# Two bias adds of a pipelined ViT-layer kernel: from selecting-row matmuls to accumulating DMAs of GpSimd, with the engines' lists ordered anew

## The chip, the cores and the metric

The kernel runs on one core of one Trainium2 chip. The metric is the device time of one execution in microseconds (us), and lower is better. All times in this document are in us unless marked ns.

## The reference

The input is a map of 64 steps x 128 rows x 64 complex states. A state-space kernel K of 1024 values for each row (computed from log_dt, B and A) is multiplied in and gives tokens `h` of 1024 values; a class token row is put beside the 128 rows. Each token then goes through an adapter (down to 128, two passes of a gated scan layer, up to 1024) and a mixture layer:

```python
h = x @ w_down.T + b_down            # after a layer norm of x; 1024 -> 128, then gelu
h = _hydra(h, *hp)                   # short causal convolution, decays, scan forward and backward,
                                     # gate silu(z), root-mean-square norm, out projection
h = alpha * xmid + (1.0 - alpha) * h
h = xmid + h
h = h @ w_up.T + b_up                # up layer, its bias is b_up
return x_init + jnp.transpose(h, (1, 0, 2))
...
base_out = jnp.einsum('btd,od->bto', x, base_W) + base_b     # base layer, its bias is base_b
logits = jnp.einsum('btd,nd->btn', x, router_W) + router_b   # 15 logits, softmax, top 8, 8 experts of rank 16
```

The output is the adapter's residual stream plus the base layer and the routed low-rank experts, computed from a second layer norm.

## The kernel before

The tokens are cut into 65 tiles of 128 (two rows of 64 steps each, `p` is the parity of the tile; the last is the class token). After a start-up block that turns and splits the weights (about 200 us), one loop body `body(i, p)` runs on each engine for i = 0 to 69, written out as straight code with a hardware loop over i = 8 to 61. It is software-pipelined over five tiles: in iteration i the engines build tile i (`A`), run the scan layer's first half for tile i-1 (`H`) and second half for tile i-2 (`G`), the up layer, residual and second norm for tile i-4 (`D`), and the base layer, router and experts for tile i-5 (`E`). What one iteration does on an engine is a list of helper calls written by hand in one order; every engine works in program order, and helpers wait on counting semaphores (`wait(eng, tile, name=count)`, `inc(ins, name)`).

What the change and the prediction touch:

- TensorE (PE): `bases(h, a, b)` multiplies parts a to b (128 of the 1024 inputs each, three 512-column matmuls a part) of the base layer into bank `bO[h]`; `route(a, b)` does the same for the expert and router columns with three 144-column matmuls a part; `lora(h)` adds the experts; `up(h)` is one half of the up layer. Before, `bases` and `up` opened their bank with a matmul of `row_sel` (two rows of ones) by `base_bias` or `up_bias`. `mix` multiplies the scan matrix `Mt` by `XS` and waits for `Mt`.
- VectorE (DVE): `gated_a` scales `XM`, the adapter input of tile i-4; `mix_matrix` writes `Mt`; `residual(h)` adds the up layer's bank to `T2` into `HB`; `final(h)` adds `bO[h]` into `HB`.
- SyncE (SP): `store` writes `HB` out after both `final`; behind it in SP's queue are the two fetches for the next iteration's `D` tile, `T2` (tokens, 512 KB) and `XM` (64 KB), whose completion is the semaphore `fetched`. `gated_a` waits for both fetches (`fetched=2`).
- GpSimd (POOL): `root_y`, `root_1`, `root_2` are powers of -0.5 for the norms, `add_bc` adds convolution taps, `carry_h` normalizes `T`, `decays_back` builds one side of the decays.

Of the kernel before, what the change touches and what calls it, by code (L numbers as in the profile page):

```python
# [26 lines left out]
ALU = mybir.AluOpType  # L27
# [27 lines left out]
def build(nc, x, cls_tok, log_dt, tok_B, inv_A_real, A_imag, w_down, b_down, w_up, b_up, gate1, in_w,  # L55
# [19 lines left out]
    with ExitStack() as keep:  # L75
# [55 lines left out]
        with ExitStack() as tmp:  # L131
# [325 lines left out]
            def _(dve):  # L457
# [128 lines left out]
                for c in range(CHUNKS):  # L586
# [89 lines left out]
                   fetched=(2, 16), up=2, h1=2, st2=4, rs2=1, nm2=1, xh2=1, tr2=2, xhi=2, xlo=2,  # L676
# [34 lines left out]
        def active(i, lag, count):  # L711
            return (not isinstance(i, int)) or 0 <= i - lag < count
# [22 lines left out]
        with nc.Block() as block:  # L735
# [64 lines left out]
            def _(pool):  # L800
                def body(i, p):
                    A, A1, D = active(i, 0, CLS), active(i, 0, TILES), active(i, 4, TILES)
                    H, G = active(i, 1, TILES + 2), active(i, 2, TILES + 2)
                    q, r, td = i - 1, i - 2, i - 4
# [97 lines left out]

                    swap()
                    kernel_q()
# [4 lines left out]
                    root_y()  # L909
                    root_1()  # L910
                    add_bc(1)
                    deviation_1()
                    add_bc(2)
                    add_bc(3)
                    add_bc(4)
                    root_2()
                    add_bc(5)
                    decays_back(0)
                    add_bc(6)
                    decays_back(1)  # L920
                    carry_h()
# [5 lines left out]
            def _(act):  # L927
# [3 lines left out]
                def body(i, p):  # L931
# [153 lines left out]

                    keep_x()
                    keep_xs()
                    exp_decays()
# [10 lines left out]
                    keep_y()  # L1099
                    exp_router()  # L1100
                    gated_hi()
# [3 lines left out]
                    exp_dt()  # L1105
# [3 lines left out]
                    scale_bc(4)  # L1109
                    scale_bc(5)  # L1110
# [3 lines left out]
                    keep_w()  # L1114
                    norm_2()
                    keep_turned(1)
# [11 lines left out]
            def _(dve):  # L1128
                TT, TS, STT = dve.tensor_tensor, dve.tensor_scalar, dve.scalar_tensor_tensor

                def body(i, p):
# [289 lines left out]
                    kernel_p()  # L1421
                    gram(0)
                    gram(1)
                    kernel_sum()
                    gram_forth()
                    gram_sum()
                    mix_matrix()
# [13 lines left out]
                    gated_a()  # L1441
                    router(0)
                    stats_1(1)
                    router(1)
                    layer_out()
                    gated_b()
                    stats_1(2)
                    conv(4, 0)
                    router(2)
                    gated_lo()  # L1450
                    stats_1(3)
                    router(3)
                    conv(4, 1)
                    conv(5, 0)
                    router(4)
                    router(5)
                    softplus(0)
                    softplus(1)
                    residual(0)
                    router(6)  # L1460
                    softplus(2)
                    shift_1()
                    softplus(3)
                    router(7)
                    stats_2(0)
                    residual(1)
                    softplus(4)
                    stats_2(1)
                    softplus(5)
                    softplus(6)  # L1470
                    conv(5, 1)
                    stats_2(2)
                    softplus(7)
                    softplus(8)
                    router(8)
                    softplus(9)
                    softplus(10)
                    softplus(11)
                    stats_2(3)
                    conv(6, 0)  # L1480
                    softplus(12)
                    shift_2()
                    conv(6, 1)
                    split_decays(0)
                    weighted_lo()
                    split_decays(1)
                    decays_forth(0)
                    decays_forth(1)
# [9 lines left out]
            def _(pe):  # L1498
                mm, tr = pe.matmul, pe.transpose

                def body(i, p):
# [6 lines left out]
                    def ffn(c0, c1, bank, ks, last=None):  # L1508

                        for k in ks:  # L1510
                            for n, (xs_, ws) in enumerate(((XHI, w_hi), (XHI, w_lo), (XLO, w_hi))):
                                ins = mm(bank[:, 0:c1 - c0], xs_[:, 1 - p, k, :], ws[:, k, c0:c1],  # L1512
                                         start=(c0 == HID and k == 0 and n == 0), stop=(last == k and n == 2))
                        return ins
# [31 lines left out]
                    def up(h):  # L1546
                        if D:
# [6 lines left out]
                            mm(bT[:, :], row_sel[:, :], up_bias[:, c], start=True, stop=False)  # L1554
                            mm(bT[:, :], GTS[:, 0, :], wu_hi[:, c], start=False, stop=False)
# [163 lines left out]
                    grams()  # L1719
                    turn_xs()  # L1720
                    decay_sums()
                    turn_x()
                    bases(0, 0, 1)
                    route(0, 1)
                    bases(1, 0, 1)
                    bases(1, 1, 2)
                    route(1, 2)
                    bases(0, 1, 2)
                    route(2, 3)
                    route(3, 4)  # L1730
                    mix()
                    s4d(0)
                    route(4, 5)
                    project_x()
                    route(5, 6)
                    s4d(1)
                    route(6, 7)
                    route(7, 8)
                    bases(0, 2, 3)
                    bases(0, 3, 4)  # L1740
                    turn_y()
                    bases(0, 4, 5)
                    bases(1, 2, 3)
# [4 lines left out]
                    bases(1, 3, 4)  # L1748
                    bases(0, 6, 7)
                    up(1)  # L1750
                    project_z()
                    bases(1, 4, 5)
                    turn_a(0)
                    bases(0, 7, 8)
                    bases(1, 5, 6)
                    turn_h()
                    bases(1, 6, 7)
                    turn_a(1)
                    bases(1, 7, 8)
# [36 lines left out]
```

How the kernel before makes its waits and increments, by code:

```python
    def after(self, eng, n, j=None):  # L48
        if isinstance(n, int) and n < 0:
            return
        j = self.per if j is None else j
        eng.wait_ge(self.sem, (n * self.per + j) * self.unit)
# [178 lines left out]
            @block.sync  # L231
# [22 lines left out]
                small(dtb[:, :], dt_bias.unsqueeze(0).broadcast_to([P, NH]))  # L254
                small(alog[:, :], A_log.unsqueeze(0).broadcast_to([P, NH]))
                small(Dbc[:, :], hy_D.unsqueeze(0).broadcast_to([P, NH]))
                small(bdn[:, :], b_down.unsqueeze(1))
                small(gate[:, :], gate1.broadcast_to([P, 1]))
                sp.wait_ge(s_zero, 3)
                for k in range(2):
                    small(bc_s[32 * k:32 * k + DST, :], in_w[2 * DIN + DST * k:2 * DIN + DST * (k + 1), :])
                    small(cwb[32 * k:32 * k + DST, :], cwr[DIN + DST * k:DIN + DST * (k + 1), :])
                    small(cbb[32 * k:32 * k + DST, :], conv_b[DIN + DST * k:DIN + DST * (k + 1)].unsqueeze(1))
                for c in range(CHUNKS):
                    sp.wait_ge(s_tab, 2 * c + 2)
                    sp.wait_ge(s_vals, 4 * c + 4)
                    sp.dma_start(tables[c * HCH // 2:(c + 1) * HCH // 2].rearrange("t f b k -> f t b k"),
                                 tab[:, c % 2, :, :].rearrange("f (t b) k -> f t b k", b=2)).then_inc(s_kept[c % 2], 16)
                for k in range(2):
                    sp.wait_ge(s_kept[k], 16 * CHUNKS // 2)
# [428 lines left out]
        def inc(ins, name):  # L700
            ins.then_inc(S[name].sem, S[name].unit)
```

## Time and profile before

| what | value |
|---|---|
| median of 3 runs | 2343.29 us (2339.07 to 2344.38) |
| the profiled execution's own time | 2339.94 us |
| its span in the trace | 2338.2 us |
| TensorE busy in the span | 2161.3 us (92%) |
| DVE, ACT, POOL busy | 1847.3, 1528.2, 1091.2 us |

TensorE's 92% is an average over a start-up of some 200 us, in which it does little, and the tile loop. The loop is read by itself in the views below. A matmul's "busy" time in the trace includes its pipeline depth, so the time that one takes from the next is the distance of two starts, not the duration printed.

### The profile page before, as it was taken

What the parts mean: (1) busy time and instruction counts of PE and PEld (TensorE: products, weight loads), DVE (VectorE), ACT (ScalarE), POOL (GpSimd) and SP (SyncE); (2) the same over time, 40 slices, a digit from 0 to 9 for tenths busy, and PEclk for the clock granted to TensorE, in tenths of its full rate; (3) what the DMA queues carried; (4) which work ended last, traced back from release to release, by engine and by line L of the source; (5) the groups of instructions that cost most, each with busy time, mean ns of one, the idle gap of its engine ahead of it and who ended that gap; (6) DMA issues with size and microseconds to landing.
All of it is one profiled execution on the core that took longest, in us unless ns stands there. A gap on an engine that the chain in (4) does not pass through costs nothing.

```text
span 2338.2 us, 51899 instructions
## 1 busy us (share of the span) xinstructions
PE 2161.3 (92%) x14117; PEld 1805.6 (77%) x14117; DVE 1847.3 (79%) x4980; ACT 1528.2 (65%) x2921; POOL 1091.2 (47%) x1350
## 2 busy tenths in 40 slices
PE   1356799999999999999999999999999999999998
PEld 1245688888888888888888888888888888888776
DVE  6847688888888888888888888888888888888764
ACT  2546576766677766667666767666777666676652
POOL 2534355444455444455444554444554444554331
PEclk9756799999999999999999999999999999999999
DMA  4400122112222122221122221122211222211211
GB/s 92 117 29 24 35 64 64 42 54 63 63 63 61 35 61 63 63 63 48 47 63 63 63 63 40 55 63 63 63 58 36 63 63 63 63 47 47 69 39 33
DMA packets 90061, 132.61 MB, mean 57 GB/s; under 512 B 20379, under 2 KB 63559, under 8 KB 90006
## 3 DMA queue, kind: packets, MB, share of 16 engines
q1 hardware_dynamic: 79176, 125.60, 18.2%
q10 hardware_dynamic: 10830, 6.35, 1.1%
q8 instruction: 25, 0.41, 0.1%
q14 instruction: 30, 0.25, 0.0%
HBM read 55.17 MB, written 76.74 MB: 56 GB/s over the span
## 4 chain that ended last, share of the span: by engine, by line
issue 43%; PE 27%; POOL 9%; DVE 7%; ACT 6%; POOLq 1%; DVEq 0%; ACTq 0%; DMA 0%; SPq 0%
PE bank L1611 5%; PE bank L1512 5%; POOL CB L901 4%; PE bank L1567 3%; PE bank L1542 2%; DVE NF L1241 2%; ACT L1006 2%; POOL XD L852 2%; PE bank L1685 1%; PE bank L1669 1%; POOL RS L886 1%; PE bank L1544 1%; PE bank L1543 1%; POOL RS L865 1%; PE bank L1659 1%
## 5 line engine op out<-in xcount | busy, mean ns | idle before, releaser
L1512 PE MATMUL bank<-w_hi,XHI 128*128 128x512 f32 (+1 forms) x1560 | 622.9, 399 | 0.0
L1512 PE MATMUL bank<-w_lo,XHI 128*128 128x512 f32 (+1 forms) x1560 | 554.7, 356 | 0.0
L1512 PE MATMUL bank<-w_hi,XLO 128*128 128x512 f32 (+1 forms) x1560 | 554.4, 355 | 0.0
L1147 DVE SCALAR_TENSOR_TENSOR CX<-bank,cw,CX 128x252 f32<-128x252 f32 (+5 forms) x804 | 335.7, 460 | 61.8 <-ACT CX L944 61.6
L901 POOL TENSOR_TENSOR CB<-CB,CM 48x252 f32<-48x252 f32 (+5 forms) x402 | 292.7, 728 | 153.6 <-ACT CM L929 142.7
L1512 PEld LDWEIGHTS bank<-w_hi,XLO 128*128 128x128 f32 x1560 | 295.5, 189 | 46.9
L1512 PEld LDWEIGHTS bank<-w_lo,XHI 128*128 128x128 f32 x1560 | 296.8, 190 | 41.4
L1512 PEld LDWEIGHTS bank<-w_hi,XHI 128*128 128x128 f32 x1560 | 296.4, 190 | 41.2
L929 ACT ACTIVATE T<-bank 64x512 f32<-64x512 f32 x256 | 151.4, 592 | 261.1 <-PE bank L1601 256.5
L865 POOL TENSOR_TENSOR RS<-VE,half_neg 128x1 f32<-128x1 f32 x65 | 35.5, 546 | 369.9 <-DVE VE L1339 369.9
L892 POOL TENSOR_TENSOR RB<-m_gt,AS 128x512 fp32r<-128x512 f32 x134 | 164.9, 1231 | 56.8 <-DVE AS L1413 56.8
L929 ACT ACTIVATE CM<-CR,cwb 48x256 f32<-48x256 f32 x402 | 181.5, 497 | 3.7 <-POOL CB L901 1.5
L859 POOL TENSOR_TENSOR RS<-MS,half_neg 128x2 f32<-128x2 f32 x67 | 46.9, 700 | 242.8 <-DVE MS L1270 242.8
L1601 PE MATMUL bank<-VB,W 128*128 128x256 f32 x512 | 148.9, 415 | 7.4 <-DVE W L1212 5.2
L1395 DVE TENSOR_TENSOR XLO<-bank,XHI 128x512 fp32r<-128x512 f32 x130 | 89.9, 692 | 72.1 <-ACT XHI L929 72.1
L1401 DVE TENSOR_TENSOR RF<-m_lt,AS 128x512 fp32r<-128x512 f32 x134 | 142.9, 1105 | 0.0
L1611 PE MATMUL bank<-XHT,wdT 128*128 128x128 f32 x1040 | 135.8, 287 | 4.5 <-ACT XHT L929 4.5
L929 ACT ACTIVATE XHI<-bank 128x512 fp32r<-128x512 f32 x130 | 77.6, 597 | 94.7 <-PE bank L1567 94.7
L1611 PEld LDWEIGHTS bank<-XHT,wdT 128*128 128x128 f32 x1040 | 129.4, 203 | 6.1 <-ACT XHT L929 6.1
L844 POOL TENSOR_TENSOR NB<-GB,sp_dt 128x512 f32<-128x512 f32 x67 | 95.9, 1431 | 77.4 <-DVE GB L1224 77.4
L852 POOL TENSOR_TENSOR XD<-XS,DD 128x512 f32<-128x512 f32 x67 | 84.6, 1263 | 99.0 <-DVE DD L1232 54.2
L1601 PEld LDWEIGHTS bank<-VB,W 128*128 128x128 f32 x512 | 89.9, 196 | 23.1 <-issue 5.9
(295 smaller groups left out, 5332.5 us busy)
## 6 DMA issues: line engine op xcount, KB each, us to landing
carried<-T SPq DMA_DIRECT2D x65, 512.0 KB, 4.8
T<-carried SPq DMA_DIRECT2D x65, 512.0 KB, 3.9
out<-HB SPq DMA_DIRECT2D x129, 256.0 KB, 3.2
tables<-tab SPq DMA_DIRECT2D x8, 560.0 KB, 4.3
TB<-tables SPq DMA_DIRECT2D x64, 70.0 KB, 2.7
carried<-U SPq DMA_DIRECT2D x65, 64.0 KB, 3.6
XM<-carried SPq DMA_DIRECT2D x65, 64.0 KB, 4.8
XI<-in_x SPq DMA_DIRECT2D x128, 32.0 KB, 2.8
```

The lines of the kernel that those rows point to most:

```text
L844: inc(pool.tensor_tensor(NB[:, :, :].rearrange("p (a h) t -> p a h t", a=2), GB[:, :, :].unsqueeze(2).broadcast_to([P, 2, NH, CS]), dtB, A ...
L852: inc(pool.tensor_tensor(XD[:, :, :], v3(XS[:, :], HD), DD[:, :].unsqueeze(2).broadcast_to([P, 2 * NH, HD]), ALU.mult), "xd")
L892: inc(pool.tensor_tensor(RB[:, part, :, :], m_gt[:, :].unsqueeze(1).broadcast_to([P, 2 * NH, CS]), decays(1, part), ALU.mult), "rb")
L901: inc(pool.tensor_tensor(CB[:, :, s:CS], CB[:, :, s:CS], CM[:, s % 3, :, 0:CS - s], ALU.add), "cbc")
L929: inc(act.activation(dst, src, ACT.Copy, scale=scale), name)
L1147: inc(STT(CX[:, c, :, s:CS], src[:, :, 0:CS - s], cw[:, c, k:k + 1], CX[:, c, :, s:CS], ALU.mult, ALU.add), "conv")
L1395: inc(TT(XLO[:, p, ks, :], v3(bT[:, :], P), XHI[:, p, ks, :].bitcast(F32), ALU.subtract), "xlo")
L1401: inc(TT(RF[:, part, :, :], m_lt[:, :].unsqueeze(1).broadcast_to([P, 2 * NH, CS]), decays(0, part), ALU.mult), "rf")
L1512: ins = mm(bank[:, 0:c1 - c0], xs_[:, 1 - p, k, :], ws[:, k, c0:c1], start=(c0 == HID and k == 0 and n == 0), stop=(last == k and n == 2))
L1567: ins = tr(bT[:, P * k:P * (k + 1)], T2[:, (4 * g + k) * P:(4 * g + k + 1) * P], ident[:, :])
L1601: ins = mm(bK[:, 256 * s:256 * (s + 1)], W[:, b, 2 * s:2 * s + 2, :].rearrange("p a c -> p (a c)"), VB[:, b, :, :].rearrange("p a c -> p ( ...
L1611: ins = mm(bK[:, 0:P], wdT[:, k, :], XHT[:, k, :], start=(k == 0), stop=(k == KC - 1))
```

## The change

Each of the two biases is now added by a DMA that GpSimd issues with an accumulating write: `bias_up` adds `b_up`, broadcast over 128 partitions, into `T2` once that is fetched; `bias_base` adds `base_b` into `HB` once the second norm has read it. `residual` waits for the first (`upb=1`), `final` for the second (`baseb=1`). The four selecting-row matmuls of an iteration go. The lists of GpSimd, ScalarE, VectorE and TensorE are written in a new order; SyncE's list is as it was. The start-up work that builds `row_sel`, `up_bias` and `base_bias` stays.

```diff
+                    def bias_up():
+                        if D:
+                            wait(pool, td, fetched=2)
+                            apart(pool)
+                            inc(pool.dma_start(T2[:, :], b_up.unsqueeze(0).broadcast_to([P, HID]), accum_op=ALU.add), "upb")
+
+                    def bias_base():
+                        if E:
+                            wait(pool, te, xh2=1)
+                            apart(pool)
+                            inc(pool.dma_start(HB[:, 1 - p, :], base_b.unsqueeze(0).broadcast_to([P, HID]),
+                                               accum_op=ALU.add), "baseb")
...
                     root_y()
+                    bias_base()
+                    bias_up()
                     root_1()
...
                     def residual(h):
-                            wait(dve, td, up=h + 1, fetched=2)
+                            wait(dve, td, up=h + 1, upb=1)
...
                     def final(h):
-                            wait(dve, te, o=h + 1)
+                            wait(dve, te, o=h + 1, baseb=1)
...
                     gram_sum()
+                    gated_a()
                     mix_matrix()
...
-                                mm(bO[h][:, :], row_sel[:, :], base_bias[:, HALF * h:HALF * (h + 1)], start=True, stop=False)
...
-                            mm(bT[:, :], row_sel[:, :], up_bias[:, c], start=True, stop=False)
-                            mm(bT[:, :], GTS[:, 0, :], wu_hi[:, c], start=False, stop=False)
+                            mm(bT[:, :], GTS[:, 0, :], wu_hi[:, c], start=True, stop=False)
```

VectorE's list, in the first body of the hardware loop, before the change, from the sum of the scan matrix (`NF`) to the first products that read `XM`:

```order
L1247 TENSOR_TENSOR NF<-NF,NB 128x512 [waits nb,nf]
L1254 TENSOR_TENSOR Mt<-NF,EX 128x512 [waits yy,ex,ns]
L1206 TENSOR_TENSOR W<-XTC,TB 128x2x192 [waits km,xtc]
L1232 TENSOR_TENSOR DD<-bank,Dbc 128x8 [waits xd,gram]
...
L1331 BN_STATS ST<-T 128x6 [waits hev]
L1352 TENSOR_SCALAR XM<-XM,al 128x128 [waits fetched]
L1297 TENSOR_TENSOR LG<-bank,rbias 128x15 [waits se,rt]
```

and the same place now:

```order
L1238 TENSOR_TENSOR GF<-bank,m_lt 128x2x63 [waits nf,nb,gram]
L1241 TENSOR_TENSOR GB<-bank,m_gt 128x2x63 [waits nf,nb,gram]
L1210 TENSOR_TENSOR VB<-TB 128x512 [waits km,x_in_even]
L1258 TENSOR_TENSOR NF<-GF,sp_dt 128x512 [waits mm,outp,g4]
L1216 TENSOR_TENSOR VB<-VB,V 128x512 [waits v1,v2]
L1264 TENSOR_TENSOR NF<-NF,NB 128x512 [waits nb,nf]
L1369 TENSOR_SCALAR XM<-XM,al 128x128 [waits fetched]
L1271 TENSOR_TENSOR Mt<-NF,EX 128x512 [waits yy,ex,ns]
L1223 TENSOR_TENSOR W<-XTC,TB 128x2x192 [waits km,xtc]
```

The scaling of `XM` (`gated_a`) moved from behind the convolution taps to the place right ahead of `Mt` (`mix_matrix`); the six instructions ahead of it are those that stood ahead of `Mt` before, in another order.

GpSimd's list around the power for the output norm (`RS<-MS`, `root_y`), before:

```order
L852 TENSOR_TENSOR XD<-XS,DD 128x512 [waits yn,tyn,dd,xse]
L859 TENSOR_TENSOR RS<-MS,half_neg 128x2 [waits yn,ms]
L865 TENSOR_TENSOR RS<-VE,half_neg 128x1 [waits sd1,xh1,st1]
L901 TENSOR_TENSOR CB<-CB,CM 48x4x63 [waits cbm]
L873 TENSOR_SCALAR SD<-RS 128x1 [waits rs1,tt]
```

and now:

```order
L852 TENSOR_TENSOR XD<-XS,DD 128x512 [waits yn,tyn,dd,xse]
L859 TENSOR_TENSOR RS<-MS,half_neg 128x2 [waits yn,ms]
L894 DMA HB<-in_L_ffn_base_b 128x1024 [waits xh2]
L887 DMA T<-in_L_attn_b_up 128x1024 [waits fetched]
L865 TENSOR_TENSOR RS<-VE,half_neg 128x1 [waits sd1,xh1,st1]
```

The two DMAs stand between `root_y` and `root_1`, the base layer's first (names are printed without buffer numbers: `T` there is `T2`).

TensorE's list just ahead of `mix` (the `Mt` row), now:

```order
L1634 MATMUL bank<-ident,XI 128x128
L1635 MATMUL bank<-ident,XSW 128x128
L1529 MATMUL bank<-w_hi,XHI 128x512
L1529 MATMUL bank<-w_lo,XHI 128x512
L1529 MATMUL bank<-w_hi,XLO 128x512
L1529 MATMUL bank<-w_hi,XHI 128x144
...
L1712 MATMUL bank<-XS,Mt 64x64 x16
```

Between `lora` and `mix` there stood two selecting-row matmuls, four base parts and four router parts; now five base parts and two router parts stand there, and the turning of `XI` comes three base parts and a router part later.

## Rows read from the trace of the kernel before

**Rows 1.** The page: span, and busy time of each engine

```profile
span 2338.2 us, 51899 instructions
PE 2161.3 (92%) x14117; PEld 1805.6 (77%) x14117; DVE 1847.3 (79%) x4980; ACT 1528.2 (65%) x2921; POOL 1091.2 (47%) x1350
```

**Rows 2.** Busy time in a stretch of the tile loop, then granted clock, DMA share

```profile
core 0: us, PE busy (x) PEld busy (x) DVE busy (x) ACT busy (x) POOL busy (x), PEclk, DMA share, GB/s
1000.00:1500.00 500.00, 497.34 (x3346) 418.81 (x3345) 414.41 (x1132) 348.12 (x665) 248.39 (x298) 1.00 0.20 59
```

**Rows 3.** Timeline of PE over one iteration: start, duration, line, operation

```profile
1000.33 0.60 PE L1578 MATMUL bank<-ident,H 128*128 128x128 f32 x4
...
1003.90 0.40 PE L1512 MATMUL bank<-w_hi,XLO 128*128 128x512 f32 x1
1004.37 0.50 PE L1542 MATMUL bank<-lb_hi,HWS 128*128 128x512 f32 x1
...
1005.87 0.60 PE L1567 MATMUL bank<-ident,T 128*128 128x128 f32 x4
...
1015.80 0.28 PE L1512 MATMUL bank<-w_hi,XHI 128*128 128x144 f32 x1
1015.91 0.28 PE L1512 MATMUL bank<-w_lo,XHI 128*128 128x144 f32 x1
...
1016.23 1.15 PE L1697 MATMUL bank<-XS,Mt 64*64 64x64 f32 x32
...
1027.57 0.51 PE L1554 MATMUL bank<-up_bias,row_sel 128*128 128x512 f32 x1
...
1030.00 0.39 PE L1554 MATMUL bank<-up_bias,row_sel 128*128 128x512 f32 x1
1030.23 0.39 PE L1555 MATMUL bank<-wu_hi,GTS 128*128 128x512 f32 x1
...
1032.48 0.60 PE L1578 MATMUL bank<-ident,H 128*128 128x128 f32 x4
```

**Rows 4.** Timeline of DVE in the same iteration

```profile
1007.74 1.28 DVE L1419 TENSOR_TENSOR HB<-bank,HB 128x512 f32<-128x512 f32 x2
...
1013.37 1.21 DVE L1247 TENSOR_TENSOR NF<-NF,NB 128x512 f32<-128x512 f32 x1
1014.72 0.69 DVE L1254 TENSOR_TENSOR Mt<-NF,EX 128x512 f32<-128x512 f32 x1
...
1024.69 0.27 DVE L1352 TENSOR_SCALAR XM<-XM,al 128x128 f32<-128x128 f32 x1
...
1029.03 0.69 DVE L1368 TENSOR_TENSOR HB<-bank,T 128x512 f32<-128x512 f32 x1
```

**Rows 5.** Timeline of SP's queue in the same iteration

```profile
1009.24 1.23 SPq L793 DMA_DIRECT2D out<-HB  x2
1010.97 0.36 SPq L759 DMA_DIRECT2D T<-carried  x1
1011.51 0.58 SPq L760 DMA_DIRECT2D XM<-carried  x1
```

**Rows 6.** DMA issues of the run: count, KB, median us to landing

```profile
T<-carried SPq DMA_DIRECT2D x65, 512.0 KB, 3.9
...
TB<-tables SPq DMA_DIRECT2D x64, 70.0 KB, 2.7
...
XM<-carried SPq DMA_DIRECT2D x65, 64.0 KB, 4.8
...
T<-in_cls_tok SPq DMA_DIRECT2D x1, 512.0 KB, 5.7
```

**Rows 7.** Timeline of POOL in the same iteration, idle time and releaser in brackets

```profile
1020.98 0.70 POOL L859 TENSOR_TENSOR RS<-MS,half_neg 128x2 f32<-128x2 f32 x1 [3.53 <-DVE MS L1270]
1027.31 0.55 POOL L865 TENSOR_TENSOR RS<-VE,half_neg 128x1 f32<-128x1 f32 x1 [5.63 <-DVE VE L1339]
```

**Rows 8.** Timeline of SP's queue at the class-token tile

```profile
2167.09 0.38 SPq L768 DMA_DIRECT2D carried<-T  x1
2167.57 0.42 SPq L748 DMA_DIRECT2D T<-in_cls_tok  x1
```

More of the change, by code:

```diff
@@ L915, in body @@
                     add_bc(4)
+                    add_bc(5)
+                    add_bc(6)
                     root_2()
-                    add_bc(5)
                     decays_back(0)
-                    add_bc(6)
+                    carry_h()
                     decays_back(1)
-                    carry_h()
                 iterations(pool, body)
@@ L1109, in body @@
                     scale_bc(4)
+                    exp_dt()
                     scale_bc(5)
@@ L1114, in body @@
                     keep_w()
+                    keep_turned(1)
                     norm_2()
-                    keep_turned(1)
                     silu_x()
@@ L1440, in body @@
                     stats_1(0)
-                    gated_a()
+                    stats_1(1)
+                    gated_b()
+                    layer_out()
                     router(0)
-                    stats_1(1)
+                    stats_1(2)
                     router(1)
-                    layer_out()
-                    gated_b()
-                    stats_1(2)
+                    gated_lo()
+                    stats_1(3)
                     conv(4, 0)
                     router(2)
-                    gated_lo()
-                    stats_1(3)
+                    conv(4, 1)
                     router(3)
-                    conv(4, 1)
-                    conv(5, 0)
                     router(4)
                     router(5)
+                    router(6)
                     softplus(0)
+                    residual(0)
                     softplus(1)
-                    residual(0)
-                    router(6)
+                    shift_1()
+                    conv(5, 0)
+                    residual(1)
+                    router(7)
+                    router(8)
+                    stats_2(0)
                     softplus(2)
-                    shift_1()
+                    stats_2(1)
                     softplus(3)
-                    router(7)
-                    stats_2(0)
-                    residual(1)
+                    conv(5, 1)
                     softplus(4)
-                    stats_2(1)
                     softplus(5)
+                    stats_2(2)
                     softplus(6)
-                    conv(5, 1)
-                    stats_2(2)
+                    stats_2(3)
                     softplus(7)
+                    conv(6, 0)
                     softplus(8)
-                    router(8)
                     softplus(9)
+                    shift_2()
                     softplus(10)
+                    weighted_lo()
                     softplus(11)
-                    stats_2(3)
-                    conv(6, 0)
                     softplus(12)
-                    shift_2()
-                    conv(6, 1)
                     split_decays(0)
-                    weighted_lo()
                     split_decays(1)
                     decays_forth(0)
+                    conv(6, 1)
                     decays_forth(1)
@@ L1512, in ffn @@
                                 ins = mm(bank[:, 0:c1 - c0], xs_[:, 1 - p, k, :], ws[:, k, c0:c1],
-                                         start=(c0 == HID and k == 0 and n == 0), stop=(last == k and n == 2))
+                                         start=(k == 0 and n == 0), stop=(last == k and n == 2))
                         return ins
@@ L1719, in body @@
                     grams()
+                    decay_sums()
+                    bases(1, 0, 1)
                     turn_xs()
-                    decay_sums()
+                    bases(0, 0, 1)
+                    bases(1, 1, 2)
+                    route(0, 1)
                     turn_x()
[L1723 to L1726, printed above, removed]
+                    bases(0, 1, 2)
                     route(1, 2)
-                    bases(0, 1, 2)
-                    route(2, 3)
-                    route(3, 4)
+                    bases(1, 2, 3)
                     mix()
                     s4d(0)
+                    bases(0, 2, 3)
+                    route(2, 3)
+                    project_x()
+                    route(3, 4)
                     route(4, 5)
-                    project_x()
+                    s4d(1)
+                    bases(0, 3, 4)
                     route(5, 6)
-                    s4d(1)
                     route(6, 7)
-                    route(7, 8)
-                    bases(0, 2, 3)
-                    bases(0, 3, 4)
                     turn_y()
                     bases(0, 4, 5)
-                    bases(1, 2, 3)
+                    route(7, 8)
                     project_out()
@@ L1748, in body @@
                     bases(1, 3, 4)
+                    bases(1, 4, 5)
+                    up(1)
                     bases(0, 6, 7)
-                    up(1)
                     project_z()
-                    bases(1, 4, 5)
                     turn_a(0)
-                    bases(0, 7, 8)
[L1755 to L1759, printed above, removed]
+                    bases(1, 5, 6)
+                    bases(1, 6, 7)
+                    bases(1, 7, 8)
+                    turn_h()
+                    turn_a(1)
+                    bases(0, 7, 8)
                     lora(0)
```

21 lines of the change are left out of this document (10 added, 11 removed).

## The prediction

> **What bounds the kernel now.** I read the page first for the engines' shares, then a stretch of the tile loop by itself, then one iteration on each engine, and last the DMA landings. The page gives TensorE 92% of the span and VectorE 79% [rows 1]. In a stretch of 500 us inside the loop TensorE is busy for 497.3 us at the full granted clock (1.00, the 2.4 GHz level), VectorE for 414 us, ScalarE 348, GpSimd 248 [rows 2]. So TensorE's own list sets the pace, and the others wait for it. One iteration lasts 1032.48 - 1000.33 = 32.15 us, from one turning of `H` to the next [rows 3]. TensorE is not wholly free of waits: `lora` starts 0.47 us after the last base matmul where two 512-column matmuls start 0.23 us apart, so about 0.2 us of each iteration is a wait for VectorE's `HWS` [rows 3].
>
> The reader should keep three distances in mind. From the end of `lora` (1005.87, where the turning of `T` starts) TensorE needs 10.36 us to reach `mix` at 1016.23 [rows 3]. VectorE finishes `Mt` at 1014.72 + 0.69 = 1015.41, so `mix` has 0.8 us to spare today [rows 3, 4]. And `gated_a` scales `XM` only at 1024.69 [rows 4], long after the fetch that SP issues at 1011.51 [rows 5] has landed, 4.8 us later in the median [rows 6].
>
> **What is removed.** Four selecting-row matmuls of 512 columns, two in `up` and two in `bases`. The one at 1030.00 is followed by the next start at 1030.23 [rows 3]: 0.23 us each, 0.94 us an iteration (the four taken at 0.235). Where such a matmul follows a group of another kind its start distance is longer (1027.57), but the matmul behind it inherits that. VectorE's weighted experts (`HWS`) move ahead of the splitting of the decays and a base part now stands last ahead of `lora`, so I also credit the 0.2 us wait. If nothing else ended later, an iteration would take 32.15 - 0.94 - 0.2 = 31.0 us.
>
> **What `gated_a` costs in its new place.** It waits for both fetches, and it now stands ahead of `mix_matrix`, so behind it on VectorE stand `Mt`, the shift products that `s4d` waits for, the skip scale, `add_skip` and the gate, that is, everything that leads to `mix` and to the output norm. The six instructions ahead of it are the old ones permuted, so VectorE gets there when it got to the end of the `NF` sum, 1013.37 + 1.21 = 1014.6 [rows 4]. SP cannot fetch sooner than now: its list is unchanged, and the two fetches queue behind the store, which waits for both `final`s (1007.74 + 1.28 = 1009.02); the store goes at 1009.24, `T2` at 1010.97, `XM` at 1011.51 [rows 4, 5]. All of this hangs on the end of `lora`, through the turning of `T`, its copy and VectorE's `XLO`, and the lists keep that order. So `XM` lands at 1011.51 + 4.8 = 1016.3. Then 0.27 us for the scaling, 0.69 us for `Mt` and about 0.1 us on each side: `mix` can start at 1017.4, 11.5 us after `lora`'s end.
>
> TensorE arrives earlier. Between `lora` and `mix` it loses two selecting-row matmuls (0.47 us); two router parts leave (six 144-column matmuls, 0.11 us apart by the starts at 1015.80 and 1015.91, 0.66 us) and one base part comes (three at 0.23, 0.69 us) [rows 3]. That is 10.36 - 0.47 + 0.03 = 9.9 us. It waits 11.5 - 9.9 = 1.6 us. `s4d` and `mix` are in order behind this and nothing later makes it up, since VectorE, POOL and ACT start their next work from `mix`. The iteration becomes 31.0 + 1.6 = 32.6 us, 0.45 us more than now. Over the 60 iterations in which the scan, the up layer and the base layer are all in work (i = 5 to 64) that is +27 us. In the filling and draining iterations TensorE has few base parts and other chains set the end; I cost those at nothing. If the landing were at 4.2 us instead of 4.8, the sum would be -9 us; at 5.4 it would be +63.
>
> **The two DMAs.** The issue itself falls into a hole. POOL finishes `root_y` at 1020.98 + 0.70 = 1021.7 and is then idle for 5.63 us until `root_1` is released [rows 7]. No row shows what a DMA issue costs on GpSimd. Below, it is SP's 0.36 us [rows 5]; above, both must fill the hole before `root_1` is late, 2.8 us each. I take 0.6 us each, near SP's rows, and nothing on the path. `bias_base` is wanted by `final` some 18 us later, so its landing costs nothing.
>
> `bias_up` is the tight one. It is issued second, and `residual(0)` wants it at 1029.03 in today's clock [rows 4], 7.3 us after `root_y`'s end. `up(0)` starts at 1027.57 [rows 3] and loses its 0.23 us, but VectorE gets to `residual(0)` only slightly earlier than now, so I allow 7.1 us from the first issue. Late by more than that, `residual(0)` holds `up(1)` on TensorE (it waits for `h1`), the router's sums, `shift_1`, `norm_1` and the next turning, one for one. The nearest row is the class token's load: 512 KB, the same broadcast of one 4 KB row over 128 partitions, issued 0.48 us behind another 512 KB DMA, landing 5.7 us after its issue [rows 6, 8]. With one issue of 0.6 us ahead that gives 6.3 us: in time by 0.8. That row is of a plain copy. An accumulating write has to read `T2` or `HB` as well. A plain 512 KB fetch lands after 3.9 us and a 70 KB one after 2.7 [rows 6], so 442 KB are worth 1.2 us and 512 KB 1.4; a second read of that size for each of the two DMAs makes 6.3 + 2.8 = 9.1 us, 2.0 us late, +120 us over 60 iterations. Both ends stand in the range. I take the plain copy's row, since it is the only one with this source and a DMA queued ahead.
>
> The Trainium skill speaks against that choice: "Collectives: The Full Stack", section "The bandwidth ceiling: the fold count and why AG ≠ RS ≠ AR", says that an adding transfer emits two source reads where a copy emits one, both on the same read ring, and so moves half the bytes a second; no row of this trace has an accumulating DMA. By its rule the sum would be the late end, about 2490. The Trainium skill's page "DMA: Bandwidth & Descriptors", section "Anatomy of one DMA — SWDGE (gpsimd) path", fits a GpSimd DMA by 2.0 us plus its bytes at 436 GB/s; by an estimate from that fit the pair with doubled reads would take 6.8 us plus the first issue, right at the limit.
>
> **The sum.** Per iteration -0.94 (matmuls) -0.2 (`HWS` wait) +1.6 (`XM`) +0.0 (issue, landing) = +0.45 us, times 60 = +27. The profiled execution took 2339.9 us, its span 2338.2; with the change 2367. The median of the runs stands 3.4 above the profiled one: 2370, and 2372 with a little for the bias DMAs' traffic beside others.
>
> **The rivals.**
> - *Both waits* (0.38): `XM` and a late `bias_up`. For it: the extra read, and two DMAs one behind the other. Against it: the class-token row is itself slowed by traffic around it. From barely late to 2.0 us late it gives 2385 to 2490; were the accumulating rate lower still, more.
> - *No wait at `gated_a`, the full saving* (0.12): this ends on the other side. The mechanism: the wait for `XM` is 1.6 us only if the fetch lands 4.8 us after its issue; if it lands by 3.2 us (1014.7), `gated_a` passes at once. The `XM` fetch lands later than the eight times larger `T2` fetch ahead of it [rows 6], so it is slowed by what shares the queues; a `final` about 1.6 us earlier against `mix` would do as well. Then an iteration takes 31.0 to 31.1 us, and the time is 2343 - 1.1 x 60 = 2277. It decides from a combined shift of 1.6 us on; the point where the kernel breaks even is a wait of 1.14 us instead of 1.6.
> - *A partial wait that just cancels the saving* (0.06): 2339 to 2348.
> - *`XM` alone* (0.44), my forecast: 2350 to 2385.
>
> **How the numbers follow.** What a measurement of this kernel can tell from no change is about 0.2%, 4.7 us. Slower by more: 0.44 + 0.38 less a sliver of each, 0.81. Within 0.2%: 0.06. Faster: 0.13. The range of 8 in 10 runs from 2335 to 2485: it holds the partial wait, my forecast and the both-waits case but for its last 0.08, and leaves out the full saving (0.12).
>
> **What the profile of the changed kernel would show.** VectorE's `XM` scaling with an idle time of about 1.6 us ahead of it, released by a DMA, right ahead of `Mt`; TensorE idle ahead of `mix` (released by `Mt`) by the same amount, so that its busy share in the loop falls from 99.5% to about 95%; 32.6 us from one turning of `H` to the next; `lora` no longer behind a wait for `HWS`. If `bias_up` is late, `residual(0)` is released by a DMA and `up(1)` by `HB`. I am wrong in sign if `XM` lands ahead of VectorE's arrival, and wrong in size by 1 us an iteration for each microsecond that `bias_up` lands later than 7.1 us after the first issue.

## The result, and the profile after

| | before | after |
|---|---|---|
| median of 4 runs | 2342.18 us | 2470.88 us (2461.75 to 2471.77) |
| ratio | | 1.0542, 95% interval 1.0514 to 1.057 |
| profiled execution, its span | 2339.94, 2338.2 us | 2470.55, 2468.8 us |

The change makes the kernel 5.4% slower, 129 us. It lies inside the forecast range (2335 to 2485) and on the forecast side, but the forecast value, 2372, had only 30 us of it.

The page of the changed kernel, busy time of each engine, DMA queues and what was read from HBM:

```profile
span 2468.8 us, 51958 instructions
PE 2143.9 (87%) x13857; PEld 1767.0 (72%) x13857; DVE 1770.1 (72%) x4980; ACT 1524.2 (62%) x2921; POOL 1169.0 (47%) x1480
...
q0 software_dynamic: 18720, 68.17, 14.9%
...
HBM read 123.33 MB, written 76.74 MB: 81 GB/s over the span
```

TensorE has 260 matmuls less (4 x 65) and 17 us less of busy time than in [rows 1], while the span is 131 us longer: it waits. The chain that ended last names for what, by line:

```profile
DMA T<-in_L_attn_b_up 17%; DMA XM<-carried 11%; DVE HB L1436 3%; POOL XD L852 3%; SPq L793 3%; PE bank L1529 2%; DVE CX L1164 2%; ACT XHI L946 2%; DVE HB L1385 1%; SPq L759 1%; POOL CB L916 1%; PE bank L1616 1%; POOL HB L894 1%; DVE ST L1392 1%; DVEq L52 1%
```

The same stretch of the loop as [rows 2] (busy time of PE, PEld, DVE, ACT, POOL, then granted clock, DMA share, GB/s), and the waits from 800 to 1500 us (total us, times, longest us):

```profile
1000.00:1500.00 500.00, 463.76 (x3055) 384.00 (x3054) 375.58 (x1082) 328.66 (x631) 247.92 (x310) 0.99 0.34 84
```

```profile
DVE XM L1369 <- DMA XM<-carried: 53.3, 20, 3.2
...
PE bank L1712 <- DVE Mt L1271: 33.5, 20, 2.2
...
PEld bank L1570 <- DVE HB L1385: 16.6, 20, 1.7
...
DVE HB L1385 <- DMA T<-in_L_attn_b_up: 15.2, 18, 1.7
```

TensorE's share falls from 99.5% to 93%. In about 20 iterations VectorE waits 2.7 us each for the `XM` fetch, TensorE 1.7 us each for `Mt` behind it, VectorE 0.8 us for the DMA that adds `b_up`, and the weights of the second half of `up` 0.8 us for the residual. One iteration shows the first wait; VectorE's timeline, with idle time and releaser in brackets, answers to [rows 4]:

```profile
1022.45 0.68 DVE L1264 TENSOR_TENSOR NF<-NF,NB 128x512 f32<-128x512 f32 x1
1025.84 0.29 DVE L1369 TENSOR_SCALAR XM<-XM,al 128x128 f32<-128x128 f32 x1 [2.71 <-DMA XM<-carried]
1026.04 0.68 DVE L1271 TENSOR_TENSOR Mt<-NF,EX 128x512 f32<-128x512 f32 x1
1026.64 0.55 DVE L1223 TENSOR_TENSOR W<-XTC,TB 128x384 f32<-128x384 f32 x1
```

TensorE's timeline of the same iteration (end of `lora`, then `mix`, then `s4d`), as in [rows 3]:

```profile
1015.30 0.60 PE L1582 MATMUL bank<-ident,T 128*128 128x128 f32 x4
...
1024.81 0.40 PE L1529 MATMUL bank<-w_hi,XLO 128*128 128x512 f32 x1
1026.87 1.15 PE L1712 MATMUL bank<-XS,Mt 64*64 64x64 f32 x32 [1.66 <-DVE Mt L1271]
1028.24 1.10 PE L1616 MATMUL bank<-VB,W 128*128 128x256 f32 x4 [0.22 <-issue]
```

`mix` starts 11.57 us after `lora`'s end, where the prediction had 11.5. GpSimd's timeline with the two DMAs, against [rows 7], and their landings (count, KB, median us from issue to landing), against [rows 6]:

```profile
1031.81 0.70 POOL L859 TENSOR_TENSOR RS<-MS,half_neg 128x2 f32<-128x2 f32 x1 [3.05 <-DVE MS L1287]
1032.46 0.92 POOL L894 DMA_DIRECT2D HB<-in_L_ffn_base_b  x1
1033.09 1.19 POOL L887 DMA_DIRECT2D T<-in_L_attn_b_up  x1
1037.76 0.57 POOL L865 TENSOR_TENSOR RS<-VE,half_neg 128x1 f32<-128x1 f32 x1 [3.48 <-DVE VE L1356]
```

```profile
T<-in_L_attn_b_up POOLq DMA_DIRECT2D x65, 512.0 KB, 7.2
HB<-in_L_ffn_base_b POOLq DMA_DIRECT2D x65, 512.0 KB, 5.1
...
XM<-carried SPq DMA_DIRECT2D x65, 64.0 KB, 4.8
```

The issues cost GpSimd about 0.6 us (the distance of their two starts) and 1.2 us, and lie in its hole, which still leaves 3.5 us idle. The up bias lands 0.63 + 7.2 = 7.8 us after the first issue; the limit was put at 7.1 us.

For the experiments I divided each iteration at six marks on TensorE: the turning of `T` behind `lora`, `mix`, the first `s4d`, `project_x`, `up(0)` and `up(1)` (of each, the first matmul that reads `GTS`, the up layer's input). The table has the mean distance of those starts in us, over the 44 to 48 iterations between 500 and 2000 us of each profiled run:

| kernel | lora to mix | mix to s4d | s4d to project_x | project_x to up(0) | up(0) to up(1) | up(1) to lora | iteration | time, us |
|---|---|---|---|---|---|---|---|---|
| before | 10.29 | 1.08 | 1.26 | 9.33 | 2.32 | 7.79 | 32.07 | 2342 |
| after | 11.63 | 1.44 | 2.23 | 8.27 | 2.77 | 7.82 | 34.16 | 2471 |
| e1_gated_back | 9.92 | 1.10 | 1.95 | 8.25 | 2.86 | 7.84 | 31.93 | 2332 |
| e2_up_first | 11.48 | 1.39 | 2.22 | 8.28 | 2.19 | 7.71 | 33.26 | 2416 |
| e3_both | 9.92 | 1.11 | 1.94 | 8.27 | 2.19 | 7.69 | 31.12 | 2276 |
| e4_old_lists_dma | 9.83 | 1.17 | 1.49 | 8.95 | 2.61 | 8.38 | 32.43 | 2365 |
| e5_new_lists_matmul | 11.55 | 1.35 | 1.93 | 8.61 | 2.32 | 7.57 | 33.32 | 2413 |
| e6_old_lists_up_first | 9.83 | 1.16 | 1.48 | 8.95 | 2.21 | 8.25 | 31.90 | 2327 |
| e7_plain_copy | 11.50 | 1.40 | 2.45 | 8.27 | 2.19 | 7.70 | 33.52 | 2424 |
| e8_xm_first | 9.98 | 1.13 | 1.94 | 8.36 | 2.19 | 7.70 | 31.29 | 2290 |
| e9_both_xm_first | 9.96 | 1.11 | 1.95 | 8.35 | 2.18 | 7.71 | 31.25 | 2285 |
| e10_new_lists_gated_back_matmul | 10.39 | 1.11 | 1.94 | 8.61 | 2.32 | 7.57 | 31.95 | 2322 |

(The new lists have a base part between `s4d` and `project_x` where the old ones have none, so those two columns compare only within old or new lists.)

### The profile page after: what moved, and what is told of

It reads as the page before. It is cut to its first block, busy times and chain, and to the rows that moved or that the text cites. A ratio compares the mean times of both kernels' runs of the same rounds, so it can differ in the third digit from the quotient of the medians.

```text
span 2468.8 us, 51958 instructions
## 1 busy us (share of the span) xinstructions
PE 2143.9 (87%) x13857; PEld 1767.0 (72%) x13857; DVE 1770.1 (72%) x4980; ACT 1524.2 (62%) x2921; POOL 1169.0 (47%) x1480
## 3 DMA queue, kind: packets, MB, share of 16 engines
q1 hardware_dynamic: 79176, 125.60, 17.2%
## 4 chain that ended last, share of the span: by engine, by line
DMA 28%; issue 26%; DVE 16%; PE 9%; POOL 7%; SPq 5%; ACT 4%; DVEq 1%; POOLq 0%; ACTq 0%
DMA T<-in_L_attn_b_up 17%; DMA XM<-carried 11%; DVE HB L1436 3%; POOL XD L852 3%; SPq L793 3%; PE bank L1529 2%; DVE CX L1164 2%; ACT XHI L946 2%; DVE HB L1385 1%; SPq L759 1%; POOL CB L916 1%; PE bank L1616 1%; POOL HB L894 1%; DVE ST L1392 1%; DVEq L52 1%
## 5 line engine op out<-in xcount | busy, mean ns | idle before, releaser
L916 POOL TENSOR_TENSOR CB<-CB,CM 48x252 f32<-48x252 f32 (+5 forms) x402 | 263.8, 656 | 203.1 <-ACT CM L946 164.2
L1712 PE MATMUL bank<-XS,Mt 64*64 64x64 f32 x2144 | 83.5, 231 | 108.5 <-DVE Mt L1271 108.5
L1616 PE MATMUL bank<-VB,W 128*128 128x256 f32 x512 | 156.9, 434 | 19.8 <-DVE W L1229 13.6
L1712 PEld LDWEIGHTS bank<-XS,Mt 64*64 64x64 f32 x2144 | 75.7, 144 | 135.0 <-issue 135.0
L1385 DVE TENSOR_TENSOR HB<-bank,T 128x512 f32<-128x512 f32 x130 | 89.9, 692 | 81.4 <-DMA T<-in_L_attn_b_up 45.9
L1369 DVE TENSOR_SCALAR XM<-XM,al 128x128 f32<-128x128 f32 x65 | 18.6, 286 | 164.9 <-DMA XM<-carried 164.9
L828 POOL TENSOR_TENSOR WI<-XTC,TB 128x384 f32<-128x384 f32 x64 | 55.7, 870 | 164.3 <-ACT XTC L946 164.3
```

The source lines that it names most:

```text
L916: inc(pool.tensor_tensor(CB[:, :, s:CS], CB[:, :, s:CS], CM[:, s % 3, :, 0:CS - s], ALU.add), "cbc")
L1616: ins = mm(bK[:, 256 * s:256 * (s + 1)], W[:, b, 2 * s:2 * s + 2, :].rearrange("p a c -> p (a c)"), VB[:, b, :, :].rearrange("p a c -> p ( ...
L1712: ins = mm(bX[rows, HD * k:HD * (k + 1)], Mt[rows, k, :], XS[rows, HD * k:HD * (k + 1)], start=True, stop=True)
```

## The experiments

**Theory 1**: two separate waits, for the `XM` fetch at `gated_a` and for the up bias at `residual(0)`, take more than the matmuls give. **Theory 2**: the accumulating DMAs themselves, by issue and traffic, are the loss, the wait for `XM` included. A third: the new order alone is the loss.

### e1: gated_a back behind stats_1(0)

```diff
                     gram_sum()
-                    gated_a()
                     mix_matrix()
...
                     stats_1(0)
+                    gated_a()
                     stats_1(1)
```

> The changed kernel with one line moved back: gated_a (the scaling of XM, which waits for the fetch) stands behind stats_1(0) again, as before the change. Theory 1 (the wait for XM ahead of Mt is the larger loss, with the waits of s4d and project_x that follow from a late Mt): the 1.7 us ahead of mix and the 0.7 us behind it go, 2.4 us x 62 = 150 us, so about 2320 us; what stays is the late bias_up. Theory 2 (the accumulating DMAs themselves are the loss: late landing, their issue on GpSimd, their traffic slowing the XM fetch): the wait moves elsewhere and the time stays near 2440 us.

Measured 2332.18 us (2331.01 to 2337.61), ratio to before 0.9957 (0.9941 to 0.9974): 139 us less than the changed kernel. `lora` to `mix` falls by 1.71 us, and the two distances behind `mix` by 0.34 and 0.28. The expectation was 2320. The single move accounts for more than the whole slowdown. Theory 2, which had the time near 2440, fails here: the DMAs are all still there, and the `XM` wait did not move elsewhere. What is left of it is the late up bias, next.

### e2: the up bias issued first

```diff
                     def bias_base():
                             wait(pool, te, xh2=1)
+                            wait(pool, te - 1, baseb=1)
...
                     root_y()
+                    bias_up()
                     bias_base()
-                    bias_up()
                     root_1()
```

> The changed kernel with bias_up issued ahead of bias_base (and bias_base waiting in addition for the bias_base of the tile before, long landed). Theory 1: bias_up no longer queues behind the base bias, lands some 2.7 us sooner than now after the first issue, and the 0.6 us wait ahead of up(1) goes: 0.6 x 62 = 35 us, about 2435 us; the wait for XM stays. Theory 2: most of the loss goes, below 2380 us.

Measured 2415.79 us (2405.86 to 2426.48), ratio 1.0315 (1.0274 to 1.0356): 55 us less than the changed kernel, where 35 were expected. `up(0)` to `up(1)` falls from 2.77 to 2.19 us, `lora` to `mix` stays at 11.5. The landings, count, KB and median us:

```profile
T<-in_L_attn_b_up POOLq DMA_DIRECT2D x65, 512.0 KB, 5.1
HB<-in_L_ffn_base_b POOLq DMA_DIRECT2D x65, 512.0 KB, 7.2
```

They have changed places: whichever goes second lands 7.2 us after its issue. For the base bias that costs nothing: from 500 to 2000 us of e3, which has the same order, no wait for it is listed.

### e3: both

> Both edits together. Theory 1: the two waits are separate and add up, 2471 - 150 - 35 = about 2285 us, below the kernel before (2342) by the four matmuls: 0.94 us x 62 = 58 us. Theory 2: the DMAs' issue and traffic keep it above 2342 us.

Measured 2276.3 us (2275.25 to 2277.68), ratio 0.9712 (0.9696 to 0.9728). The two waits are separate and add up: 2470.9 - 138.7 (e1) - 55.1 (e2) = 2277.1, measured 2276.3. That the two agree within 1 us is partly luck, since e2's four runs lie 20 us apart; e1 less e3, with runs within 7 us, gives 55.9 us for the late up bias as well. With both gone the change is worth 66 us, 2.9%, the fastest kernel of this study. Its page, and the stretch of [rows 2], in which TensorE is as full as before the change:

```profile
span 2275.9 us, 51985 instructions
PE 2097.2 (92%) x13857; PEld 1750.0 (77%) x13857; DVE 1778.9 (78%) x4980; ACT 1524.9 (67%) x2921; POOL 1188.2 (52%) x1480
```

```profile
1000.00:1500.00 500.00, 497.40 (x3356) 416.89 (x3355) 412.42 (x1174) 359.31 (x692) 276.56 (x339) 1.00 0.38 92
```

### e4 and e6: the old lists with the DMAs

Both leave every list of the kernel before as it was, take the four matmuls out and put the two DMAs behind `root_y`; e4 with the base bias first, e6 with the up bias first.

```diff
                     root_y()
+                    bias_base()      # e6: bias_up() first, and bias_base's extra wait as in e2
+                    bias_up()
                     root_1()
```

> The kernel before with all its lists as they were, and only the biases exchanged: the four selecting-row matmuls out, bias_base and then bias_up issued right behind root_y. Theory 1: no wait for XM; the matmuls give 0.94 us and the late bias_up takes 0.5 to 0.7 us back, about 2325 us. Theory 2: as slow as the changed kernel or nearly, above 2400 us. A third theory (the new order of the lists is the whole loss and the DMAs are free): about 2285 us.

Measured 2364.75 us (2360.79 to 2370.92), ratio 1.0095 (1.0073 to 1.0117): slower than before, by 22 us, and 40 above what theory 1 gave. So the third theory fails: without any reordering the DMAs do not give their saving. Against e6 below, the late up bias costs these lists 38 us, less than the 55 of the new ones. The 40 us above theory 1 are therefore not the bias: e6 misses by the same amount.

> The lists of the kernel before, the biases by DMAs behind root_y, bias_up ahead of bias_base (bias_base waits in addition for the one of the tile before). Theory 1: bias_up lands 5.1 us after its issue, ahead of residual(0), so every trace of the wait goes, also the 0.6 us that e4_old_lists_dma lost behind up(1): 32.07 - 0.94 = 31.1 us an iteration, about 2283 us. If the 0.6 us come from the issue on GpSimd or from traffic, they stay: about 2320 us.

Measured 2326.66 us (2325.95 to 2333.29), ratio 0.9945 (0.9927 to 0.9963): 44 above theory 1. The wait at `residual(0)` is gone (2.21), yet 0.46 us of the 0.94 saved are given back between `up(1)` and `lora` (7.79 to 8.25). The waits of e6 from 800 to 1500 us say for what in part:

```profile
PEld bank L1559 <- DVE HWS L1298: 17.3, 22, 0.8
...
PE bank L1559 <- DVE HWS L1298: 7.7, 22, 0.4
```

In the old lists VectorE writes `HWS` behind the splitting of the decays; TensorE, now faster, arrives at `lora` before it. From the start of the last base matmul to that of `lora` it takes 0.47 us before the change, 0.75 us in e4 and e6, 0.40 in e3 and 0.28 in e10 in the mean. So 0.28 of the 0.77 us that e6 gives back are this wait, which the new lists do not have. Another 0.30 us go between `mix` and `project_x` (1.16 + 1.48 against 1.08 + 1.26), for which no wait of a matmul is listed. That the matmuls' saving needs the new order is shown by e6 against e3; that it is the move of `HWS` alone was not tried.

### e5 and e10: the new lists with the matmuls

e5 has all four lists in the new order, with the selecting-row matmuls and without any DMA of GpSimd; e10 also has `gated_a` back.

> All four lists in the new order, but the biases added by the four selecting-row matmuls as before the change, and no DMA from GpSimd. Theory 1 (gated_a's wait for XM sets when mix can start, whatever adds the biases): lora's end to mix stays 11.5 us as in e2_up_first, and the other 21.8 us of its iteration gain the two matmuls of up, 0.47 us: 33.26 + 0.47 = 33.7 us, about 2445 us, some 100 above the kernel before. Theory 2 (the DMAs' traffic and issue cause the wait): 2342 us or below.

Measured 2413.01 us (2410.06 to 2414.05), ratio 1.0302 (1.0285 to 1.0319). The expectation was 32 us too high, but the sign and the place are theory 1's: without a single DMA on GpSimd, `lora` to `mix` is 11.55 us and the kernel is 71 us slower than before. Its waits:

```profile
DVE XM L1352 <- DMA XM<-carried: 53.4, 21, 3.2
...
PE bank L1697 <- DVE Mt L1254: 22.6, 21, 1.6
```

VectorE waits as long as in the changed kernel. TensorE waits 1.1 us instead of 1.7 (1.5 in e2), since its selecting-row matmuls fill part of the time: removing them ahead of a `mix` that comes late gains nothing there. e2, the same lists with the DMAs and without the late up bias, takes 2416 us, no less than e5's 2413: with `gated_a` in this place the exchange of matmuls for DMAs is worth nothing.

> All lists in the new order but gated_a at its old place, and the biases by the four selecting-row matmuls. Theory 1: this is e3_both with the four matmuls back, 0.94 us x 65 = 61 us more: 2276 + 61 = about 2337 us, the kernel before within 0.3%. If the new order is worth something by itself with TensorE full, it is below 2330; if the DMAs cost something hidden in e3_both, it is nearer to 2300.

Measured 2322.18 us (2320.11 to 2332.88), ratio 0.9929 (0.9908 to 0.9951): the new order without `gated_a`'s move is worth 18 us, and the exchange of the matmuls for DMAs 46 us (against e3; 31.95 to 31.12 = 0.83 us an iteration), less than the 61 expected. Of the 0.94 us 0.12 come back as the wait for `HWS` ahead of `lora` (0.28 to 0.40 us). The 18 us lie for the most part outside the columns, where the pipeline fills: in the profiled executions the fourth `mix` starts at 279.4 us before the change and at 267.2 in e10, 12 us sooner; the iterations from there to the sixty-first give only 0.12 us each.

### e7: the same bytes, copied and not added

```diff
-                            inc(pool.dma_start(T2[:, :], b_up.unsqueeze(0).broadcast_to([P, HID]), accum_op=ALU.add), "upb")
+                            inc(pool.dma_start(up_bias[:, :].bitcast(F32), b_up.unsqueeze(0).broadcast_to([P, HID])), "upb")
```

and the same for `base_b` into `base_bias`, two tiles that are no longer read, each DMA waiting in addition for its own of the tile before. The output lacks both biases.

> The changed kernel, but the two DMAs of GpSimd copy the same 512 KB broadcasts into two tiles that nobody reads, with no accumulation: both biases are left out of the output, all waits stay. Theory A (an accumulating write reads its destination too, so it moves half as fast): each DMA loses 1.3 us of data time, the second lands some 4.6 us after its issue instead of 7.2, at twice the GB/s while both move, and the wait ahead of residual(0) goes: about 2416 us, as e2_up_first. Theory B (the fixed time of a GpSimd DMA, or the one-row source in HBM, makes it late): landing stays 6.5 to 7.2 us and the time near 2465 us.

Measured 2423.83 us, one run. `up(0)` to `up(1)` is 2.19 us as in e2: copied, the second DMA is in time. The landings:

```profile
up_bias<-in_L_attn_b_up POOLq DMA_DIRECT2D x65, 512.0 KB, 4.9
base_bias<-in_L_ffn_base_b POOLq DMA_DIRECT2D x65, 512.0 KB, 3.9
```

And the DMA while the pair moves, us by us, in the changed kernel (last two columns: share of the 16 engines, GB/s that they moved):

```profile
1034.00:1035.00 1.00, 1.00 (x8) 0.91 (x8) 1.00 (x4) 0.95 (x3) 0.28 (x1) 1.00 0.95 123
1035.00:1036.00 1.00, 1.00 (x8) 0.91 (x7) 1.00 (x2) 0.30 (x1) 0.00 (x0) 1.00 1.09 217
1036.00:1037.00 1.00, 1.00 (x6) 0.65 (x4) 0.61 (x3) 0.03 (x1) 0.00 (x0) 1.00 1.09 213
1037.00:1038.00 1.00, 0.95 (x7) 0.69 (x6) 1.00 (x7) 0.67 (x3) 0.24 (x1) 1.00 1.02 201
1038.00:1039.00 1.00, 1.00 (x5) 0.61 (x4) 0.90 (x6) 0.58 (x2) 0.52 (x2) 1.00 1.07 209
1039.00:1040.00 1.00, 1.00 (x6) 0.82 (x5) 0.56 (x4) 0.97 (x3) 0.13 (x1) 1.00 0.45 86
```

and in e7:

```profile
1020.00:1021.00 1.00, 1.00 (x7) 0.82 (x6) 1.00 (x3) 0.97 (x3) 0.20 (x1) 1.00 0.53 188
1021.00:1022.00 1.00, 1.00 (x12) 1.00 (x10) 1.00 (x4) 0.97 (x2) 0.00 (x0) 1.00 0.99 303
1022.00:1023.00 1.00, 1.00 (x8) 0.87 (x7) 1.00 (x4) 0.60 (x1) 0.00 (x0) 1.00 1.01 401
1023.00:1024.00 1.00, 1.00 (x7) 0.90 (x7) 0.58 (x1) 0.00 (x0) 0.00 (x0) 1.00 0.40 156
```

With all engines busy the accumulating pair moves the biases at 201 to 217 GB/s, the copying pair at 303 to 401. Over the whole pair the shares add up to 5.7 and 2.9 us of all 16 engines: the accumulating write takes 1.9 times the engine time for the same bytes. That is theory A's rate, and its size too: 7.2 against 4.9 us for the second. The Trainium skill ("Collectives: The Full Stack", section "The bandwidth ceiling: the fold count and why AG ≠ RS ≠ AR") puts an adding transfer at two source reads, and so at half the rate of a copy. This trace agrees with the half; whether the second read or the adding itself takes the time, no run here separates. The time is 8 us above e2's median and inside the span of e2's runs (2405.86 to 2426.48); see the clock, below.

### e8 and e9: XM fetched ahead of T2

```diff
-                        inc(sp.dma_start(T2[:, :], src[:, 0:HID]), "fetched")
-                        inc(sp.dma_start(XM[:, :], src[:, HID:HID + P]), "fetched")
+                        inc(sp.dma_start(XM[:, :], src[:, HID:HID + P]), "xmf")
+                        inc(sp.dma_start(T2[:, :], src[:, 0:HID]), "fetched")
```

with `gated_a` waiting for `xmf=1` and `bias_up` for `fetched=1`; e8 on e2, e9 on e3.

> e2_up_first with gated_a still ahead of Mt, but SP fetches XM (64 KB) ahead of T2 (512 KB), on a semaphore of its own. Theory 1: XM is late because it is issued 0.54 us later and queues behind 512 KB: now it lands some 3 us after an issue 0.54 us sooner, about 1.5 us of the 2.4 us wait on VectorE that counts goes, with half of the waits that follow a late Mt: about 2300 to 2330 us. If what delays it is the store ahead of both, or the write of carried<-T behind them, it stays above 2380 us.

Measured 2289.96 us (2284.9 to 2290.87), ratio 0.9774 (0.9758 to 0.979): 126 us less than e2 and 10 below the expected range, with `gated_a` still right ahead of `Mt`. Landings:

```profile
T<-carried SPq DMA_DIRECT2D x65, 512.0 KB, 4.7
...
XM<-carried SPq DMA_DIRECT2D x65, 64.0 KB, 2.4
```

Issued first, the 64 KB land after 2.4 us instead of 4.7, and 0.54 us earlier besides: 2.8 us in all, a little more than the 2.4 us (51.3 us in 21 waits) that VectorE waited for them in e2. So the wait was one for 64 KB issued behind 512 KB in one queue. What stands behind `XM` now lands later: `T2` 4.7 us after its issue instead of 3.9, and `TB` 3.3 instead of 2.7. The store ahead of both and the write behind them, the rivals that the expectation named, are unchanged.

> e3_both (gated_a at its old place, bias_up first) with XM fetched ahead of T2 as in e8_xm_first. Theory 1: gated_a already stands long behind the landing, so fetching XM sooner gives nothing: 2276 us, within 0.3%. If the T2 fetch, now landing 4.7 us after its issue and later by 0.54 us, held bias_up, it would be slower.

Measured 2285.23 us (2284.49 to 2287.71), ratio 0.9762 (0.9745 to 0.9778): not the 2276 expected, 9 us slower than e3. `project_x` to `up(0)` is 0.08 us longer and `lora` to `mix` 0.04. The only wait of a matmul that is listed from 500 to 2000 us, in e3 and then in e9:

```profile
PE bank L1652 <- DVE U L1304: 4.6, 24, 0.2
...
PE bank L1652 <- DVE U L1304: 8.6, 24, 0.4
```

The 4 us more, over 48 iterations, are the 0.08 us: in every second iteration `project_bc`, which stands between the two marks, waits longer for `U`. Why VectorE writes `U` later when `T2` and `TB` land later is not shown; it stays open.

## Why the prediction was right or wrong

The direction was right, the size was not: +30 us forecast, +129 measured. By terms: the matmuls and the `HWS` wait, -68 forecast and -64 measured (e10 and e3); the `XM` wait, +96 and +139; the late up bias, nothing and +55. The last two terms are the miss. That the first agrees so well is partly luck: 10 to 12 us of the 64 come from the filling of the pipeline (the fourth `mix` in e3 and e10), which I had "at nothing".

- **What bounds the kernel, and the period.** Right: 32.15 was 32.07 in the mean. Without the two waits I gave 31.0 us; e3 has 31.12.
- **"The wait for `HWS`", -0.2, and the four matmuls, -0.94.** Together -1.14 forecast and -0.95 measured (32.07 to 31.12). The parts: the new order gives 0.12 and the matmuls 0.83 (e10). The wait for `HWS` shrank by 0.2 us, as credited, only while the matmuls stayed (e10, 0.47 to 0.28 us); with TensorE earlier it is 0.40 (e3). What I did not see is that the 0.94 depends on the new order: in the old lists (e6) TensorE gains only 0.17 us.
- **`gated_a`, +1.6.** The mechanism, the place and the stall were right: 1.56 us (e2 less e3, `lora` to `mix`). VectorE itself waits 2.7 us where the prediction had 1.7 (1016.3 - 1014.6), since it ends the `NF` sum 7.8 us after `lora` and not 8.7; that earlier arrival only lengthens its wait. The term was undersized by what follows. I took the stall as passed on one for one ("nothing later makes it up") and put nothing on top: behind a late `Mt` the shift products come late too, so `s4d` starts another 0.28 us later, and 0.28 us in the mean go to TensorE's clock (below). In all 2.14 us an iteration, 139 us instead of 96 (1.6 x 60). The factor was short as well: 139.5 / 2.14 = 65 iterations by the medians, and 134.2 / 2.14 = 63 between the two profiled executions, from which the 2.14 is.
- **The step that failed: "I take the plain copy's row".** The row of the class-token load gave 6.3 us for the landing of the up bias after the first issue, in time by 0.8, and so a term of 0.0; it was 7.8, late by 0.7, and the term 55 us. The bound for a second read gave 9.1, and the truth lay between: each accumulating write takes 1.2 us more than a copy (e7: 5.1 against 3.9 alone, 7.2 against 4.9 behind another), but the plain pair is also faster than that row (0.63 + 4.9 = 5.5 us). Why, no run shows; the row is a single load, and it took 4.9 to 6.5 us in the other kernels of this study. With 5.5 + 2 x 1.4 = 8.3 the doubled read would have come within 0.5 us. I had a rule that spoke for doubling and a row that couldn't, since it was a plain copy, and I let the row decide a question that it doesn't touch. The limit of 7.1 was good: 7.8 is 0.7 late, and `up(0)` to `up(1)` lost 0.58, the stretches around it another 0.3 (after less e2: 0.90 us an iteration, 55 us; e1 less e3: 0.81 and 56).
- **The issue on GpSimd, 0.6 us each in the hole.** Right for the path, on the low side for the second (1.19 us).
- **The rivals.** The right one was "both waits", 2385 to 2490, which had 0.38 against my 0.44. The case on the other side (no wait at `gated_a`, 2277) is what e3 shows: its price was right within 1 us, with some luck, since a saving of 1.1 us in 60 iterations stands there for 0.95 us and the 10 us of the filling. It needed the 1.6 us to vanish, and the landing did not move: 4.8 us before and after.

The sum by the experiments: 2341 - 18 (new order, e10) - 46 (matmuls, e3) + 139 (`XM` ahead of `Mt`) + 55 (late up bias) = 2471.

## What to carry to other kernels

In a program-order engine, a small instruction moved forward brings its wait with it: before moving one, work out when what it waits for has landed, compare that with the time at which the engine will reach it in its new place, and count as well what else stands behind it on that engine. When two transfers of different size are wanted at different times, issue the one wanted first at the head of the queue, however small it is (2.4 against 4.7 us here, and the up bias before the base bias); what it overtakes lands later, so this is for a wait that sits on the path (e9 lost 9 us where no such wait was left). An accumulating DMA should be priced at about twice the transfer time of a copy (1.9 here), and a trace that has only copies bounds it only from below.

## What the runs showed of the hardware

**A late matmul can cost the clock too.** In 13 of 50 loop iterations of the changed kernel the stretch from `s4d` to `project_x` takes 2.7 to 3.6 us instead of 1.92, with no wait in it. The trace has 13 stretches of the lower granted clock in that time (400 to 2100 us), one in each of these iterations. One of them, stretch by stretch (PE, PEld, DVE, ACT, POOL busy, then the granted clock):

```profile
819.00:820.50 1.50, 0.00 (x0) 0.00 (x0) 0.94 (x3) 0.00 (x0) 0.00 (x0) 1.00 0.43 143
820.50:822.00 1.50, 1.22 (x33) 1.14 (x33) 1.05 (x3) 0.00 (x0) 0.88 (x1) 1.00 0.02 7
822.00:825.50 3.50, 3.50 (x11) 2.87 (x11) 1.39 (x2) 1.59 (x4) 0.48 (x1) 0.51 0.00 0
825.50:827.00 1.50, 1.50 (x11) 1.40 (x11) 0.17 (x1) 0.92 (x3) 0.70 (x2) 1.00 0.00 0
```

TensorE idles 2.0 us ahead of `mix`, runs the small 64x64 matmuls of `mix`, waits 0.2 us more, and then the granted clock is at its lower level (0.5, 1.2 GHz) for some 3.5 us, in which it works without a pause. In the iteration shown in the result section, with an idle time of 1.66 us, the clock stays at 1.00. The excess of that stretch over its shortest sums to 17.2 us in the changed kernel, 15.9 in e2 (11 iterations), 27.6 in e7 (19 iterations), and at most 2 in all other kernels. The 11.7 us between e7 and e2 fit the 12.0 us between their profiled executions (2423.83 and 2411.83). An idle time ahead of `mix` alone does not bring it on. In the iterations that are hit it is 1.33 to 2.30 us, in others of the same three kernels up to 2.19; and e5 idles 0.74 to 1.65 us, 1.33 or more in 9 of 51 iterations, with none hit. In the remaining kernels TensorE idles ahead of `mix` not at all, or once. What decides which iterations are hit was not tried.

**A GpSimd DMA of 512 KB** has landed 3.9 us after its issue when it copies and 5.1 us when it accumulates; a second one right behind lands 4.9 and 7.2 us after its own issue. The issue itself is shown as 0.53 to 0.64 us of GpSimd copying and 0.92 to 1.19 us accumulating; from the first start to the second end the pair takes 1.2 and 1.8 us, since the second starts some 0.63 us behind the first either way.
